# A four-layer graph network on one core: in the last layer's loop, TensorE takes the next tile's scores first in each step and turns a finished tile between the two parts of the weighted sum

## What is computed

```python
    qkv = x @ W
    q, k, v = jnp.split(qkv, [Fqk, 2 * Fqk], axis=-1)
    q = (q * scaling).reshape(n, H, Fh)
...
    aw = jnp.einsum('ehf,ehf->eh', q[src], k[dest])
    m = jax.ops.segment_max(aw, src, num_segments=n)
    e = jnp.exp(aw - m[src])
    denom = jax.ops.segment_sum(e, src, num_segments=n)
    alpha = e / denom[src]
    out = jax.ops.segment_sum(alpha[:, :, None] * v[dest], src, num_segments=n)
```

## Time and profile before

| What | Value |
|---|---|
| device time, median of 3 runs | 1310.76 us (1310.09 to 1312.12) |
| the profiled execution's own time | 1311.84 us |
| its span in the trace | 1310.1 us |
| TensorE matmuls, busy | 1178.8 us (90%) |
| VectorE, busy | 924.0 us (71%) |
| ScalarE, busy | 708.2 us (54%) |
| GpSimd, busy | 65.2 us (5%) |
| ten transposes' line in the last layer, L1243 into `wide` | 874 in the kernel, 282 ns mean |
| the maximum, L1228 | 1450 ns |
| the exponential, L797 | 1429 ns |

### The profile page before, as it was taken

One profiled execution on the slowest core, in us unless ns is written; L12 is line 12 of the kernel. 1 busy time (PEld: TensorE's weight loads), 2 busy tenths in 40 slices (PEclk: granted clock), 3 DMA queues, 4 the chain that ended last, 5 costly groups with the idle time before them and its releaser, 6 DMA issues.

```text
span 1310.1 us, 16906 instructions
## 1 busy us (share of the span) xinstructions
PE 1178.8 (90%) x5857; PEld 736.3 (56%) x5857; DVE 924.0 (71%) x1663; ACT 708.2 (54%) x885; POOL 65.2 (5%) x115
## 2 busy tenths in 40 slices
PE   4999959997998986979999999859988999999996
PEld 3666635554785544435444544434545777777775
DVE  6999873105455697778998896673116888888885
ACT  1232368202556667148778777531115777777774
POOL 3000042000001100000000000000000000000000
PEclk8999959997899996979999999979997999999999
DMA  4000000003003000201111100020011111110102
GB/s 148 5 1 1 1 1 2 1 1 129 1 1 89 2 1 1 81 23 42 42 42 42 42 23 3 1 96 1 1 24 25 25 26 25 26 25 1 26 1 79
DMA packets 24769, 36.15 MB, mean 28 GB/s; under 512 B 11874, under 2 KB 13204, under 8 KB 24694
## 3 DMA queue, kind: packets, MB, share of 16 engines
q1 hardware_dynamic: 24694, 35.14, 9.0%
HBM read 26.03 MB, written 2.70 MB: 22 GB/s over the span
## 4 chain that ended last, share of the span: by engine, by line
PE 56%; DVE 11%; ACT 5%; issue 3%; DMA 0%; SPq 0%; ACTq 0%; DVEq 0%; POOLq 0%
PE wide L58 15%; PE wide L1613 12%; PE wide L1243 7%; PE small L1697 5%; PE wide L1601 3%; PE wide L1603 3%; PE small L1655 2%; ACT arena L797 2%; PE small L1243 2%; DVE arena L1126 2%; PE wide L1402 1%; PE small L1710 1%; DVE arena L1150 1%; DVE bn L812 1%; DVE bns L915 1%
## 5 line engine op out<-in xcount | busy, mean ns | idle before, releaser
L58 PE MATMUL wide<-arena 125*125 (+7 forms) x2028 | 487.2, 389 | 33.3 <-DVE arena L873 12.6
L58 PEld LDWEIGHTS wide<-arena 125*125 (+4 forms) x2028 | 270.6, 141 | 226.7 <-issue 144.1
L1613 PE MATMUL wide<-arena 125*65 125x512 f32 (+1 forms) x480 | 181.5, 514 | 0.0
L1243 PE MATMUL small<-ident,arena 125*128 125x125 f32 (+5 forms) x438 | 85.8, 347 | 62.1 <-ACT arena L593 32.0
L1150 DVE TENSOR_TENSOR arena<-wide,arena 125x1250 f32<-125x1250 f32 x80 | 116.7, 1459 | 35.2 <-PE wide L1603 35.2
L725 ACT ACTIVATE arena<-arena,b 125x1250 f32<-125x1250 f32 x80 | 106.7, 1336 | 58.4 <-PE wide L1613 54.0
L782 ACT ACTIVATE arena<-wide 125x1000 f16<-125x1000 f32 x80 | 80.8, 1010 | 80.8 <-PE wide L1243 80.8
L1243 PE MATMUL wide<-ident,arena 125*125 125x125 f32 (+2 forms) x874 | 116.8, 282 | 6.5 <-ACT arena L797 3.5
L797 ACT ACTIVATE arena<-arena,neg_max,unit 125x1250 f32<-125x1250 f32 x80 | 114.3, 1429 | 10.5 <-DVE neg_max L1231 10.5
L1613 PEld LDWEIGHTS wide<-arena 125*65 125x65 f32 x480 | 63.1, 138 | 101.0 <-issue 94.5
L1204 DVE SCALAR_TENSOR_TENSOR arena<-wide,arena 125x1000 f16<-125x1000 f32 x80 | 95.9, 1198 | 33.8 <-ACT arena L782 33.8
(11 more groups left out here) (241 smaller groups left out, 1221.0 us busy)
## 6 DMA issues: line engine op xcount, KB each, us to landing
arena<-rows_kept SPq DMA_DIRECT2D x16, 625.0 KB, 5.6
arena<-arena SPq DMA_DIRECT2D x40, 156.2 KB, 2.8
arena<-in_L_gnn_W SPq DMA_DIRECT2D x3, 1024.0 KB, 7.6
x_nm<-in_x SPq DMA_DIRECT2D x2, 1250.0 KB
out<-x_nm SPq DMA_DIRECT2D x1, 2187.5 KB
arena<-in_L_gnn_W_l SPq DMA_DIRECT2D x1, 1024.0 KB, 5.8
arena<-in_L_gnn_W_r SPq DMA_DIRECT2D x1, 1024.0 KB, 8.1
arena<-in_L_gnn_Wk SPq DMA_DIRECT2D x1, 1024.0 KB, 5.5
```

Source lines behind the costliest of these rows:

```text
L58: mm = pe.matmul(ps[0:rows, lo:hi], lhsT, rhs[:, lo:hi], start=start, stop=stop, skip_group_check=True)
L1243: return pe.transpose(dst, src, ident[0:k, 0:k])
L1613: m = pe.matmul(psW[1][0:VA, lo:hi], v_gat[0:ROWS, t, h, :], ring[n % RINGS][0:ROWS, lo:hi], start=(t == 0), stop=(t == TILES - 1))
```

## The change

The order of three pieces in each step of TensorE's loop in the last layer. The scores of tile n + 1 come first in the step; then three blocks of the weighted sum; then the transposes of tile n - 2; then the other two blocks and, in every other step, the fold. Nothing else in the kernel is touched.

```diff
@@ -1715,13 +1715,13 @@
                 pe.wait_ge(S["acc_read"], H)
                 score(0)
                 for n in range(H * TILES + 5):
-                    if 2 <= n < H * TILES + 2:
-                        turn_tile(n - 2)
+                    if n + 1 < H * TILES:
+                        score(n + 1)
                     half = n % 2
                     if 4 <= n < H * TILES + 4:
                         weigh_pair((n - 4) // 2, (range(5 * half, 5 * half + 3)))
-                    if n + 1 < H * TILES:
-                        score(n + 1)
+                    if 2 <= n < H * TILES + 2:
+                        turn_tile(n - 2)
                     if 4 <= n < H * TILES + 4:
                         weigh_pair((n - 4) // 2, (range(5 * half + 3, 5 * half + 5)))
                     if n >= 6 and n % 2 == 0:
```

## The result

| | before | changed |
|---|---|---|
| median | 1311.44 us (4 runs, 1310.09 to 1312.67) | 1703.74 us (4 runs, 1699.31 to 1720.06) |
| ratio | | 1.3014, 95% interval 1.2926 to 1.3103 |
| the profiled execution, its span | 1311.84 us, 1310.1 us | 1706.24 us, 1704.5 us |

The change makes the kernel 30% slower. The forecast was 1699 us.

A forecast was written before the change was run, and what follows sets the result against it. TensorE was taken to bound the loop at 3.81 us a lap. Laps of 8.91 us (+387.5 over 76) and +1.1 for the ends took 1311.84 to 1700.4, less 1.1 to the median: 1699 us, range 1610 to 1770.

The forecast's parts named there:

- The ring: TensorE, ScalarE and VectorE in the loop: the chain of waits closes after one tile, 7.06 us a lap against 3.81.
- Its two signs: In the loop: scores wait for the max (L1228) in each lap, and L1228 starts right behind lower (L1206).
- A third: In the loop: lower (L1204) waits for upper (L782), and L782 for the transposes (L1243), by some 3 to 4 us.
- What was costed at nothing: Last two weighted-sum blocks and fold, add_quad, exponential and ScalarE's copy: hidden beside the chain of waits, no added time.
- The rival that was not slower: VectorE reaches the next max without waiting for lower; TensorE's 3.71 us a lap is the bound, 1304 us; chance 0.02.
- The clock: TensorE idles 3.35 us a lap, so its clock falls to 1.2 GHz in nearly every lap: 8.91 us, not 7.06.
- The return after 4.5 us: TensorE's higher clock returns 4.5 us into a lap's work: scores and first blocks slow, 0.81 us of the transposes slow.
- The two clock rivals: TensorE's clock stays at 2.4 GHz, 1559 us, chance 0.10; or never comes back in the loop, 1765 us, chance 0.14.
- the second rival: TensorE's higher clock never comes back in the loop, a third being transposes: 9.77 us a lap, 1765 us; chance 0.14.
- Head and tail: Loop's start, up to the scores of tile 3, and its end, from those of tile 79: together +1.1 us.
- S of tile 3 starts 2.26 us earlier: Loop's start: the scores of tile 3 go before the transposes of tile 0, starting 2.26 us earlier.
- In the tail: From the scores of tile 79 to the transposes of tile 79: 12.57 us in place of 9.17, so +3.4.

The follow-up runs named there:

- the idle time filled: Changed kernel plus 26 or 18 extra unread matmuls before a step's scores, and ScalarE's copy of a pair's sum moved ahead of the exponential: 1575.47 us (1.2005).
- the first experiment: Changed kernel with lower one step later on VectorE, so the max of tile n+1 stands ahead of lower of tile n-2: 1450.21 us (1.1039).
- the experiment with the shorter ring: Changed kernel with the transposes put straight behind the scores, ahead of the weighted sum's first blocks, nothing else: 1612.64 us (1.2288).

## Why the prediction was right

**The ring: right.** The step "S of n+1, Wa, T of n-2, upper, lower of n-2, max of n+1, S of n+2" holds link by link. At the higher clock it was worked out at 7.06 and measured at 7.08 with the idle time filled. Its two signs were there: the scores wait for L1228 in each lap, and L1228 starts right behind L1206. A third was off: L782 and L1204 were to wait by some 3 to 4 us and wait 6.0 and 5.4 us on average (467.3 / 78 and 420.1 / 78). Such a wait is the lap less the engine's own work, about 2.8 us on ScalarE and 3.4 on VectorE, so 3 to 4 us belongs to the ring of 7.06 us and not to the 8.91 that were forecast. What was costed at nothing (Wb, F, add_quad, the exponential, the copy) did stay beside the ring: the lap shown above is made of the ring's links alone. The rival that was not slower fell with the first experiment: only when the max is taken ahead of lower in VectorE's queue does its mechanism come into being.

**The clock: right in sum, rougher in detail.** The forecast had 8.91 us a lap and the measured mean is 8.91. Its parts: S slow 2.46 and measured 2.46; Wa slow 1.23, an estimate by the ratio of S, and measured 1.23; T to upper, all slow, 2.08 and measured 1.92. An all-slow lap is thus 9.61 and not 9.77. The return after 4.5 us was too simple a picture: in two laps of five (31 of 76) it came only when the chain's work on TensorE was all but done, or not at all; in most others it came earlier, or had fallen later. That errors on both sides cancelled is luck; the experiment with the shorter ring, worked out in the same way, was off by 0.6 us a lap. The two clock rivals are out: the clock didn't stay up (laps near 7.1 us are three of 76), and it didn't stay down, as 43 of the 74 laps with a Wa lie below 9.5 us, and all slow they would take 9.6. The rule on transposes in the Trainium skill, "TensorE: Matmul & The Clock Gate", Part 4, had spoken for the second rival. Here the clock did come back in a loop a third of whose work is transposes, and ten of them took 1.25 us at a granted 1.00 in the kernel with its idle time filled.

By the Trainium skill, "TensorE: Matmul & The Clock Gate", section "A second HAM failure mode: psum-queue depth-cycling", a kernel that pauses often between groups of matmuls swings between both clock levels and loses throughput by it. This case agrees: 0.50, 1.00 and 0.50 again in the three stretches above, and 139 us for it.

**Head and tail: small misses, 7.3 us where 1.1 was forecast.** The step "S of tile 3 starts 2.26 us earlier" failed, since it waits for the max of tile 2: it starts 996.08 - 991.84 = 4.24 us after the scores before, a gain of 0.6. In the tail, +3.4 was forecast and +7.9 measured. S to T of tile 79 took 1689.97 - 1672.89 = 17.1 us and not 12.6. S and Wa ran at the lower clock, 3.7 us in place of 1.95, and the three intervals between the last transposes took 13.4 us in place of 10.6: the first blocks of the weighted sum waited 2.48 us for L526 at 1685.12, with T queued behind them. The forecast had three intervals of 3.54 us from the kernel before, where T stood ahead of those blocks.

**What the forecast overlooked without harm.** It said nothing of the ring through the three row buffers (4.9 us a lap). The shorter ring doesn't show while a longer one is closed, so the time came out right; but a repair built on the forecast's ring alone would have gained 253 of 392 us and stopped there. It had F whole in its ring of two tiles (7.23 against 7.62 us for two laps) and was right in that; the mean share of F is a slip of the expectation for the order T, S, Wa, Wb alone.

## What to carry to other kernels

When a piece is moved in one engine's queue, write down each ring of waits that goes through it (every engine's program order counts as a link, and so does each buffer that comes free), add up its links from the trace, and divide by the number of tiles that one turn of it carries. Here the ring was 7.2 us for two tiles before and is 7.1 us for one after (with Wa in it in place of Wb and F): nearly the same length, and the division changed. A ring that is just under the bound can't be seen in the waits, and behind the longest ring there may stand a shorter one, so cut them together.

## What was not expected of the hardware

TensorE was given more work and the kernel became faster: the added matmuls kept the granted clock at 1.00, and the same chain took 7.08 us a lap in place of 8.91. With idle stretches of 2.05 to 3.6 us before the scores the clock was at 0.50 for part of 73 of the 76 laps; in the run with the order T, S, Wa, Wb the mean clock stayed at 1.00, with waits of the scores of at most 0.3 us.
